# A gather run as one stream, with other transfer shapes, and the product of a quad as one instruction

## The chip, the cores and the metric

The kernel runs on one core of a Trainium2 chip. The metric is the device time of one execution in microseconds (us), lower is better. The engines are TensorE (PE; its weight loads stand as PEld), VectorE (DVE), ScalarE (ACT), GpSimd (POOL) and SyncE (SP), which here only issues transfers to the core's 16 DMA engines.

## What is computed

The reference is a chain of four layers on x of 8 images, 256 channels, 32 x 32 points in float32, each added to x: a selective scan, a mixture of experts, three deformable stages, and a 1x1 convolution. The change is in the deformable stages. Cut to that part:

```python
def _deform(x, ow, ob):
    off = (_conv(x, ow, 1) + ob[None, :, None, None]).reshape(B, C, 2, H, W)
    py = clip(yy + off[:, :, 0], 0, H - 1); px = clip(xx + off[:, :, 1], 0, W - 1)
    y0, x0 = floor(py), floor(px); y1 = minimum(y0 + 1, H - 1); x1 = minimum(x0 + 1, W - 1)
    wy, wx = py - y0, px - x0
    # v00 = x[.., y0, x0] and so on, gathered for each channel and point
    return v00*(1-wy)*(1-wx) + v01*(1-wy)*wx + v10*wy*(1-wx) + v11*wy*wx
h = _bn(_conv(_deform(x, ow1, ob1), w1, 0), ...)     # 256 channels in, 64 out
h = _bn(_conv(_deform(h, ow2, ob2), w2, 1), ...)     # 64 channels
h = _bn(_conv(_deform(h, ow3, ob3), w3, 0), ...)     # 64 channels in, 256 out
```

Every channel has its own sampling positions py and px at each of the 1024 points.

## The kernel before

**No indices are used.** The kernel first takes differences of each image along both axes (`dense`). A sample at (py, px) is then the sum over rows i and columns j of difference(i, j) times clamp(py - i + 1, 0, 1) times clamp(px - j + 1, 0, 1). So a gather is three steps for a channel: row weights, a matmul over i, a product with the column weights, and a sum over j.

**Stages.** `kernel_program` (L1860) runs the scan layer, the experts, `build_offsets_1` (L1149), `load_constants`, and then `build_gather` (g1), `build_middle` (o2), `build_gather` (g2), `build_middle` (o3), `build_gather` (g3) and `build_last`. The offsets stages write four DRAM tensors: `dense` (image differences), `coords` (both coordinates, each split in two parts s whose sum is the float32 value), `whole` (the row coordinate unsplit), and the gather writes `gathered`.

**Quads.** A gather works on sets of 128 channels; g1 has 16 sets, g2 and g3 four each. A set has two halves of 512 points (`NH`), each with 8 quads (`QUADS`), a quad being 16 channels: four units r of 32 partitions times four channels c. So g1 has 256 quads and g2 and g3 64 each, 384 in all. For each quad q:

- Row weights `kw` (128 partitions x 4 x 512: image row on partitions): the coordinate of channel c = 0 of each unit is spread over 32 partitions by a TensorE matmul with `spread` (L1457) and read by ScalarE with a relu (L1401). The coordinates of c = 1 to 3 (`SENT`) come from `whole` by four transfers that each repeat three rows over 32 partitions (`send_rows`, L1346), three buffers deep (`SB`), and VectorE takes the relu of all three (L1423). GpSimd clamps all four at 1 (L1415).
- Row sums: 16 matmuls of 32 x 32 by 512 (L1472; each shows as two records) from `img` and `kw` into four PSUM banks.
- Column weights `vw`: four spread matmuls (L1457) and four relus of ScalarE (L1401), through a ring of three PSUM banks.
- The product (`weigh`, L1434): VectorE multiplies two of the four banks with min(vw, 1), in two instructions per quad. The row matmuls of the next quad wait for both (`weighted`).
- The fold: four matmuls with `fold` (L1482) add over j. After 8 quads ScalarE evacuates the fold bank (L1386) and SyncE stores the half set to `gathered` (L1363).

**Order.** Each engine's order is written out by hand. On VectorE it is product of quad n, then relu of quad n + 2. On TensorE it is row sums of n, three spreads, fold of n - 1, two spreads. The spreads belong to quads n + 1 (`v`) and n + 2 (`k`).

**The loop.** `build_gather` runs a loop over turns of `SETS` = 4 sets; between turns all engines meet at the end of the block. In a turn SyncE issues: rows of quad 0, the loads of set 0, rows of quads 1 and 2, the loads of sets 1, 2 and 3, and then rows of quad 3 and on, each when the relu three quads before is done. The loads of a set (`load_set`) are four transfers of coordinates, 128 partitions x 4 KB each (L1351, 2 MB in all), and after the first of them four of the image, 32 partitions x 32 pieces of 128 bytes each (L1357, 0.5 MB in all).

**The stores** of the stages before: in `build_offsets_1` SyncE stores `dense`, `coords` and `whole`; in `build_middle`, a loop of two turns of four images, per image `dense` (L1638, 64 partitions x 4 KB), two of `coords` (L1642) and `whole` (L1645).

## Time and profile before

| | us |
|---|---|
| median of 3 runs | 5976.52 (5972.13 to 5980.63) |
| the profiled execution | 5969.8, its span 5968.1 |
| TensorE busy | 4860.9 (81% of the span) |
| VectorE busy | 3608.7 (60%) |
| ScalarE busy | 1857.1 (31%) |
| GpSimd busy | 1478.1 (25%) |
| mean granted TensorE clock | 0.887 of full |

The busy shares are means over stages of very different kinds. The sum in the prediction is made against the profiled execution; the median of the runs is 6.7 us above it. A wait is put down by the profile to what ended last before it.

### The profile page before, as it was taken

The numbers are of one execution on the slowest core, as the hardware profiler recorded it, in microseconds if no ns is written. First come the engines' busy times: TensorE is split into PE (matmuls) and PEld (weight loads), VectorE is DVE, ScalarE is ACT, GpSimd is POOL, SyncE is SP. The second block draws the span as 40 slices with busy tenths as digits, with TensorE's granted clock in tenths as the row PEclk, the third lists the DMA queues.
The fourth block names the chain that finished last, engine by engine and source line by source line (L and its number), as shares of the span: only waits on it lengthen the run. The fifth ranks groups of instructions, "written<-read, shape, count | busy, mean of one in ns | idle before, by whom it ended". The sixth has DMA issues, their size and how long they took to land. (4 is left out here: it accounts for less than half of the span.)

```text
span 5968.1 us, 82574 instructions
## 1 busy us (share of the span) xinstructions
PE 4860.9 (81%) x30592; PEld 2689.8 (45%) x30592; DVE 3608.7 (60%) x4317; ACT 1857.1 (31%) x2899; POOL 1478.1 (25%) x1828
## 2 busy tenths in 40 slices
PE   4787887876999799979989994959596983985886
PEld 2333333324777677757767771313131332332222
DVE  6888888875666566652212223848484873863764
ACT  2222222202222122220000003848484751751660
POOL 0222222220000000011101002636363651642540
PEclk7888888867999899989999996979797996997988
DMA  1000000001000000011111119989898968978962
GB/s 30 15 20 17 21 22 21 15 21 65 15 15 8 22 15 15 8 61 74 43 71 74 53 67 193 217 180 218 178 220 181 217 171 183 218 145 143 221 178 91
DMA packets 377577, 558.13 MB, mean 94 GB/s; under 512 B 167464, under 2 KB 169064, under 8 KB 376264
## 3 DMA queue, kind: packets, MB, share of 16 engines
q1 hardware_dynamic: 377160, 552.64, 37.7%
q8 instruction: 253, 4.15, 0.3%
q14 instruction: 164, 1.34, 0.1%
HBM read 439.27 MB, written 113.25 MB: 93 GB/s over the span
## 5 line engine op out<-in xcount | busy, mean ns | idle before, releaser
L1415 POOL TENSOR_SCALAR g_kw<-g_kw 128x512 f32<-128x512 f32 x1536 | 960.8, 650 | 936.7 <-ACT g_kw L1401 637.1
L1401 ACT ACTIVATE g_vw<-ps,l_index 128x512 f32<-128x512 f32 x1536 | 971.0, 686 | 520.4 <-PE ps L1457 520.1
L1434 DVE SCALAR_TENSOR_TENSOR g_prod<-g_vw,ps 128x1024 f32<-128x1024 f32 x768 | 903.3, 1218 | 213.0 <-PE ps L1472 213.0
L1294 PE MATMUL ps<-o_pad,o_ow 128*128 128x512 f32 x3456 | 852.5, 409 | 8.5 <-DVE o_pad L822 7.7
L1457 PE MATMUL ps<-g_coord,l_spread 128*128 128x512 f32 x1920 | 678.5, 452 | 147.6 <-DMA g_coord<-coords 147.4
L1093 PE MATMUL ps<-l_pair,l_w 128*128 128x512 f32 x3072 | 780.3, 403 | 0.0
L1294 PEld LDWEIGHTS ps<-o_pad,o_ow 128*128 128x128 f32 x3456 | 657.3, 191 | 198.0 <-DVE o_pad L822 7.9
L1472 PE MATMUL ps<-g_kw,g_img 32*32 32x512 f32 x12288 | 458.9, 620 | 311.7 <-DVE g_prod L1434 272.5
L1457 PEld LDWEIGHTS ps<-g_coord,l_spread 128*128 128x128 f32 x1920 | 313.1, 194 | 831.1 <-ACT g_vw L1401 615.6
L1093 PEld LDWEIGHTS ps<-l_pair,l_w 128*128 128x128 f32 x3072 | 575.6, 191 | 156.6 <-issue 29.4
L1423 DVE TENSOR_SCALAR g_kw<-g_rows,l_index 128x1536 f32<-128x1536 f32 x384 | 389.8, 1015 | 416.0 <-DMA g_rows<-whole 416.0
L1401 ACT ACTIVATE g_kw<-ps,l_index 128x512 f32<-128x512 f32 x384 | 264.5, 689 | 1098.3 <-PE ps L1457 1081.6
L752 PE MATMUL ps<-l_rows_p,l_sel 72*128 72x512 bf16 x768 | 293.8, 473 | 211.0 <-DVE l_dbx L609 127.2
L1482 PE MATMUL ps<-g_prod,l_fold 128*32 128x512 f32 x3072 | 413.9, 611 | 9.5 <-DVE g_prod L1434 9.5
L1038 DVE TENSOR_TENSOR l_act<-ps,l_act 128x512 f32<-128x512 f32 x256 | 177.0, 691 | 398.0 <-ACT l_act L966 397.5
L428 POOL TENSOR_TENSOR l_acc<-l_acc,l_seen 128x1024 f32<-128x1024 f32 x112 | 283.2, 2528 | 512.9 <-DVE l_seen L619 512.9
L1105 PE MATMUL ps<-l_mixed,l_w 128*128 128x512 f32 x1536 | 401.3, 396 | 3.5 <-DVE l_mixed L822 1.9
L966 ACT ACTIVATE l_act<-ps 128x512 f32<-128x512 f32 x256 | 153.3, 599 | 776.1 <-PE ps L1093 776.1
L130 POOL TENSOR_TENSOR l_moments<-l_moments,l_minus_half 128x2 f32<-128x2 f32 x24 | 16.6, 692 | 1444.2 <-DVE l_moments L99 1444.2
L1105 PEld LDWEIGHTS ps<-l_mixed,l_w 128*128 128x128 f32 x1536 | 287.7, 188 | 79.0 <-issue 7.3
L1472 PEld LDWEIGHTS ps<-g_kw,g_img 32*32 32x32 f32 x12288 | 106.0, 104 | 468.6 <-POOL g_kw L1415 275.6
L1132 DVE SCALAR_TENSOR_TENSOR o_pos<-ps,o_ob,o_grid 128x1024 f32<-128x1024 f32 x32 | 41.1, 1283 | 442.2 <-PE ps L1294 441.9
(247 smaller groups left out, 4911.9 us busy)
## 6 DMA issues: line engine op xcount, KB each, us to landing
g_rows<-whole SPq DMA_DIRECT2D x1536, 192.0 KB, 4.4
g_coord<-coords SPq DMA_DIRECT2D x96, 512.0 KB, 7.2
coords<-o_parts SPq DMA_DIRECT2D x32, 1024.0 KB, 4.0
l_x<-xcur SPq DMA_DIRECT2D x16, 1024.0 KB, 6.5
coords<-o_parts SPq DMA_DIRECT2D x32, 512.0 KB, 5.1
g_img<-dense SPq DMA_DIRECT2D x96, 128.0 KB, 8.6
gathered<-g_res SPq DMA_DIRECT2D x48, 256.0 KB, 4.8
l_xn<-in_x SPq DMA_DIRECT2D x8, 1024.0 KB, 5.0
```

Of the source, the lines that this page charges most:

```text
L428: ins = nc.gpsimd.tensor_tensor(acc[:, h, :], acc[:, h, :], seen[:, i % 2, :], ALU.add)
L752: ins = nc.tensor.matmul(ps[:, lo:lo + HALF], sel[:, q, :], rows_p[:, mine, h, j * HALF:(j + 1) * HALF], start=True, stop=True)
L1093: ins = nc.tensor.matmul(bank(b_ + i % 2), w[:, a, k, e, f * P:(f + 1) * P], pair[:, m % 2, c, k, j * HALF:(j + 1) * HALF], start=(k == 0 ...
L1105: ins = nc.tensor.matmul(bank(5 + c), w2[:, a, f, e, c * P:(c + 1) * P], mixed2[:, i % 3, d, :], start=(e == 0 and f == 0 and r == 0), sto ...
L1294: ins = nc.tensor.matmul(ps[:, lo:lo + HALF], ow[:, a, kk, tap, y, k * P:(k + 1) * P], padded_rows(pad[:, m, c, kk], j, tap), start=(n == ...
L1401: nc.scalar.activation(to, bank(a % RING), ACT.Relu, bias=index[:, 0:1]).then_inc(sem("ring_read"), 1)
L1415: nc.gpsimd.tensor_scalar(part, part, 1.0, 0.0, ALU.min, ALU.max).then_inc(sem("clamped"), 1)
L1423: nc.vector.tensor_scalar(kw[:, q % KB, OWN:4, :].rearrange("p c n -> p (c n)"), rows[:, q % SB].rearrange("p c n -> p (c n)"), index[:, 0 ...
L1434: nc.vector.scalar_tensor_tensor(prod[:, n % PB, 2 * half:2 * half + 2, :].rearrange("p r n -> p (r n)"), vw[:, n % VB, 2 * half:2 * half ...
L1457: nc.tensor.matmul(bank(a % RING), spread[:, int(kind == "v"), h, c, :], coord[:, s, t, j * HALF:(j + 1) * HALF], start=True, stop=True).t ...
L1472: ins = nc.tensor.matmul(ps[c * SIDE:(c + 1) * SIDE, lo:lo + HALF], img[mine, s, g, c, :], kw[mine, n % KB, c, :], start=True, stop=True)
L1482: ins = nc.tensor.matmul(ps[r * SIDE:(r + 1) * SIDE, FOLD_BANK * HALF:(FOLD_BANK + 1) * HALF], fold[:, g, :], prod[:, n % PB, r, :], start ...
```

## The change

`build_gather` loses its loop: all sets of a gather are one block, and 16 sets of g1 are written out. `coord` and `img` hold two sets instead of four and are reused; the loads of set s + 1 are issued while set s runs, after the rows of its quads 7 (image), 8 to 11 (columns) and 12 (row coordinates).

The shapes of transfers change with the layout of the DRAM tensors. The image goes in as four transfers of 32 partitions x 4 KB. The coordinates go in as four transfers of columns, 16 partitions x 4 pieces of 4 KB, and four of rows, 16 partitions x 4 KB, for the two channels of each group of eight whose rows TensorE spreads. Only these row coordinates are loaded. `coord` has 80 partitions, and the spread matmuls contract over 80 rows instead of 128. `whole` holds the three sent channels next to each other, so the rows of a quad are read as one piece of 6 KB (before: three of 2 KB) for each partition, and the four quarters are issued in the order 0, 2, 1, 3. For this the channels of a quad are chosen by `channel_of`, and `spread` and `fold` are built to match.

The product of a quad is one VectorE instruction of 2048 elements over four banks, and waits for all four column weights.

The stages before store `dense` in the new layout, in pieces of 128 bytes, and `build_offsets_1` does so in two transfers per image.

```diff
-SETS = 4
+CROWS = 80
...
                             sp.wait_ge(sem("steps_ready"), KC * (m + 1))
-                            sp.dma_start(dense[bass.ds((b0 + m) * C, C), :].rearrange("(k p) n -> p k n", p=P),
-                                         x[:, m % 2]).then_inc(sem(f"stored{m}"), 16)
+                            for kk in range(KC):
+                                sp.dma_start(dense[bass.ds((b0 + m) * KC + kk, 1)].rearrange("a i p j -> (a p) i j"),
+                                             x[:, m % 2, kk, :].rearrange("p (i j) -> p i j", j=SIDE))\
+                                  .then_inc(sem(f"stored{m}"), 16)
                             if m + 2 < IMGS:
-                                sp.wait_ge(sem(f"stored{m}"), 16)
...
-                        sp.dma_start(coords[bass.ds((b0 + m) * KC + k, 1), y, :, :, :].rearrange("a s p n -> (a p) s n"),
+                        sp.dma_start(coords[bass.ds((b0 + m) * KC + k, 1), y, :, :, :].rearrange("a p s n -> (a p) s n"),
                                      co.stored(slice(0, P), i)).then_inc(sem(f"coords_stored{i}"), 16)
                         if y == 0:
-                            sp.dma_start(whole[bass.ds((b0 + m) * KC + k, 1)].rearrange("a p n -> (a p) n"),
-                                         co.pos[:, i % 2, :]).then_inc(sem(f"coords_stored{i}"), 16)
+                            sp.dma_start(whole[bass.ds((b0 + m) * KC + k, 1)].rearrange("a j p n -> (a p) j n"),
+                                         co.pos[:, i % 2, :].rearrange("p (j n) -> p j n", j=NH)).then_inc(sem(f"coords_stored{i}"), 16)
...
+def channel_of(h, c):
+
+    return h if c == 0 else 2 + 3 * h + c - 1
...
-        coord = st.sb("coord", [P, SETS, 4, N], F32R)
-        img = st.sb("img", [P, SETS, QUADS, 4, SIDE])
+        coord = st.sb("coord", [CROWS, 2, 4, N], F32R)
+        img = st.sb("img", [P, 2, QUADS // 2, 8, SIDE])
-        quads = [(s, j, g) for s in range(SETS) for j in range(NH) for g in range(QUADS)]
-        Q = len(quads)
+        rows = st.sb("rows", [P, SB, 3, HALF])
+        quads = [(s, j, g) for s in range(sets) for j in range(NH) for g in range(QUADS)]
...
-        with nc.Fori(0, blocks // SETS) as turn:
-            n0 = turn * SETS
...
+        with nc.Block() as block:
+
+            @block.sync
+            def _(sp):
+                def send_rows(q):
+                    s, j, g = quads[q]
+                    if q >= SB:
+                        sp.wait_ge(sem("sent_relu"), q - SB + 1)
+                    t, h = divmod(g, 2)
+                    for r in (0, 2, 1, 3):
+                        lo = r * SIDE + 8 * t + channel_of(h, 1)
+                        sp.dma_start(rows[r * SIDE:(r + 1) * SIDE, q % SB].rearrange("p c n -> p (c n)"),
+                                     whole[s, j, lo:lo + 3].rearrange("q n -> (q n)").partition_broadcast(SIDE))\
+                          .then_inc(sem(f"rows_sent{q % SB}"), 16)
+
+                def load_image(s):
+                    if s >= 2:
+                        sp.wait_ge(sem("rows_summed"), PER_SET * (s - 1))
+                    for r in range(4):
+                        mine = slice(r * SIDE, (r + 1) * SIDE)
+                        sp.dma_start(img[mine, s % 2].rearrange("p t q j -> p (t q j)"),
+                                     dense[s, :, mine, :].rearrange("i q j -> i (q j)")).then_inc(sem(f"img_loaded{s % 2}"), 16)
+
+                def load_columns(s, r):
+                    sp.dma_start(coord[16 * r:16 * (r + 1), s % 2].bitcast(F32),
+                                 coords[s, 1, r * SIDE:(r + 1) * SIDE].rearrange("(t q) s n -> (q s) t n", t=4))\
+                      .then_inc(sem(f"coord_loaded{s % 2}"), 16)
+
+                def load_rows(s):
+                    for t in range(4):
+                        sp.dma_start(coord[CM:CROWS, s % 2, t].bitcast(F32),
+                                     coords[s, 0].rearrange("(r t q) s n -> t r q s n", r=4, t=4)[t, :, 0:2]
+                                     .rearrange("r q s n -> r (q s) n")).then_inc(sem(f"coord_loaded{s % 2}"), 16)
+
+                def store(r):
+                    s, j = divmod(r, NH)
+                    sp.wait_ge(sem("res_ready"), r + 1)
+                    sp.dma_start(gathered[s * P:(s + 1) * P, j * HALF:(j + 1) * HALF],
+                                 res[:, r % 2, :]).then_inc(sem(f"stored{r % 2}"), 16)
+
+                send_rows(0)
+                for r in range(4):
+                    load_columns(0, r)
+                load_rows(0)
+                load_image(0)
+                send_rows(1)
+                send_rows(2)
+                for q in range(SB, Q):
+                    send_rows(q)
+                    s, part = divmod(q, PER_SET)
+                    if s + 1 < sets:
+                        if part == 7:
+                            load_image(s + 1)
+                        if 8 <= part < 12:
+                            load_columns(s + 1, part - 8)
+                        if part == 12:
+                            load_rows(s + 1)
+                    if q % QUADS == SB + 2 and q >= QUADS:
+                        store(q // QUADS - 1)
+                store(sets * NH - 1)
+                for r in range(2):
+                    sp.wait_ge(sem(f"stored{r}"), 16 * sets)
...
+                def weigh(n):
+                    dve.wait_ge(sem("rows_summed"), n + 1)
+                    if n >= PB:
+                        dve.wait_ge(sem("folded"), n - PB + 1)
+                    dve.wait_ge(sem("ring_read"), at["v", n, 3] + 1)
+                    nc.vector.scalar_tensor_tensor(prod[:, n % PB].rearrange("p r n -> p (r n)"),
+                                                   vw[:, n % VB].rearrange("p r n -> p (r n)"),
+                                                   1.0, ps[:, ROW_BANK * HALF:(ROW_BANK + 4) * HALF], ALU.min,
+                                                   ALU.mult).then_inc(sem("weighted"), 1)
+
+                for n in range(-2, Q):
+                    if n >= 0:
+                        weigh(n)
+                    if n + 2 < Q:
+                        relu(n + 2)
...
+                    if j == 0 and g == 0:
+                        pe.wait_ge(sem(f"coord_loaded{s % 2}"), 128 * (s // 2 + 1))
+                    nc.tensor.matmul(bank(a % RING), spread[:, h, c if kind == "v" else 4, :],
+                                     coord[:, s % 2, t, j * HALF:(j + 1) * HALF], start=True,
+                                     stop=True).then_inc(sem("ring_filled"), 1)
+
...
+                    if j == 0 and g == 0:
+                        pe.wait_ge(sem(f"img_loaded{s % 2}"), 64 * (s // 2 + 1))
+                    pe.wait_ge(sem("clamped"), 4 * (n + 1))
+                    if n:
+                        pe.wait_ge(sem("weighted"), n)
...
+                            ins = nc.tensor.matmul(ps[c * SIDE:(c + 1) * SIDE, lo:lo + HALF], img[mine, s % 2, g // 2, channel_of(g % 2, c), :],
+                                                   kw[mine, n % KB, c, :], start=True, stop=True)
+                    ins.then_inc(sem("rows_summed"), 1)
...
-                        sp.dma_start(dense[bass.ds(b * CM, CM), :], step[:, m, :]).then_inc(sem("stored"), 16)
+                        part = slice(m % 2 * CM, (m % 2 + 1) * CM)
+                        sp.dma_start(dense[bass.ds(turn * (PASS // 2) + m // 2, 1), :, part, :].rearrange("a i p j -> (a p) i j"),
+                                     step[:, m, :].rearrange("p (i j) -> p i j", j=SIDE)).then_inc(sem("stored"), 16)
                         sp.wait_ge(sem("coords_ready"), m + 1)
                         for y in range(2):
                             half = slice(m % 2 * CM, (m % 2 + 1) * CM)
-                            sp.dma_start(coords[bass.ds(turn * (PASS // 2) + m // 2, 1), y, :, half, :]
-                                         .rearrange("a s p n -> (a p) s n"),
+                            sp.dma_start(coords[bass.ds(turn * (PASS // 2) + m // 2, 1), y, half, :, :]
+                                         .rearrange("a p s n -> (a p) s n"),
                                          co.stored(slice(y * CM, (y + 1) * CM), m)).then_inc(sem(f"coords_stored{m}"), 16)
-                        sp.dma_start(whole[bass.ds(turn * (PASS // 2) + m // 2, 1), half, :].rearrange("a p n -> (a p) n"),
-                                     co.pos[0:CM, m % 2, :]).then_inc(sem(f"coords_stored{m}"), 16)
+                        sp.dma_start(whole[bass.ds(turn * (PASS // 2) + m // 2, 1), :, half, :].rearrange("a j p n -> (a p) j n"),
+                                     co.pos[0:CM, m % 2, :].rearrange("p (j n) -> p j n", j=NH)).then_inc(sem(f"coords_stored{m}"), 16)
...
-        dense = dram("dense", (B * C, N))
+        dense = dram("dense", (B * C // P, SIDE, P, SIDE))
         gathered = dram("gathered", (B * C, N))
-        coords = dram("coords", (B * C // P, 2, 2, P, N))
-        whole = dram("whole", (B * C // P, P, N))
+        coords = dram("coords", (B * C // P, 2, P, 2, N))
+        whole = dram("whole", (B * C // P, NH, P, HALF))
         build_scan_layer(nc, t, ps, xcur)
```

The removed code of the loop body stands in the kernel above. ScalarE's, GpSimd's and TensorE's orders stay, with `weighted` counted once per quad; the constants `spread` and `fold` follow the new channel order.

## Rows read from the trace of the kernel before

**Rows 1.** The page: span, and DMA share of each of 40 slices
```profile
span 5968.1 us, 82574 instructions
DMA  1000000001000000011111119989898968978962
```

**Rows 2.** Timeline of SyncE's queue (start us, us, engine, line, operation): stage bounds
```profile
3610.10 1.88 SPq L1346 DMA_DIRECT2D g_rows<-whole  x4
...
4875.49 2.16 SPq L1628 DMA_DIRECT2D o_x<-gathered  x4
...
5004.64 1.77 SPq L1346 DMA_DIRECT2D g_rows<-whole  x4
...
5319.34 16.09 SPq L1633 DMA_DIRECT2D o_x<-gathered  x8
...
5473.62 1.75 SPq L1346 DMA_DIRECT2D g_rows<-whole  x4
...
5787.81 0.55 SPq L1759 DMA_DIRECT2D l_h<-gathered  x1
```

**Rows 3.** Timeline of all engines, one steady quad of the first gather
```profile
3703.21 2.35 DVE L1434 SCALAR_TENSOR_TENSOR g_prod<-g_vw,ps 128x1024 f32<-128x1024 f32 x2 [0.53 <-PE ps L1472]
...
3704.87 0.74 PE L1457 MATMUL ps<-g_coord,l_spread 128*128 128x512 f32 x2
...
3705.48 1.01 DVE L1423 TENSOR_SCALAR g_kw<-g_rows,l_index 128x1536 f32<-128x1536 f32 x1
...
3705.71 1.15 PE L1472 MATMUL ps<-g_kw,g_img 32*32 32x512 f32 x32
3705.99 0.68 ACT L1401 ACTIVATE g_vw<-ps,l_index 128x512 f32<-128x512 f32 x1
...
3707.03 2.35 DVE L1434 SCALAR_TENSOR_TENSOR g_prod<-g_vw,ps 128x1024 f32<-128x1024 f32 x2 [0.53 <-PE ps L1472]
```

**Rows 4.** Timelines of VectorE and SyncE's queue, first turn's end, second turn's head
```profile
3913.29 2.35 DVE L1434 SCALAR_TENSOR_TENSOR g_prod<-g_vw,ps 128x1024 f32<-128x1024 f32 x2 [1.47 <-PE ps L1472]
...
3926.95 3.03 SPq L1346 DMA_DIRECT2D g_rows<-whole  x4
...
3933.72 1.02 DVE L1423 TENSOR_SCALAR g_kw<-g_rows,l_index 128x1536 f32<-128x1536 f32 x1 [18.09 <-DMA g_rows<-whole]
...
3949.99 1.02 DVE L1423 TENSOR_SCALAR g_kw<-g_rows,l_index 128x1536 f32<-128x1536 f32 x1 [15.25 <-DMA g_rows<-whole]
3950.92 2.35 DVE L1434 SCALAR_TENSOR_TENSOR g_prod<-g_vw,ps 128x1024 f32<-128x1024 f32 x2
...
3995.56 1.02 DVE L1423 TENSOR_SCALAR g_kw<-g_rows,l_index 128x1536 f32<-128x1536 f32 x1 [37.60 <-DMA g_rows<-whole]
```

**Rows 5.** Windows: stretch, us, busy us of engines, granted clock, DMA share, GB/s
```profile
3956.00:3995.00 39.00, 7.00 (x58) 1.96 (x56) 1.96 (x2) 6.22 (x10) 1.41 (x3) 0.59 1.10 211
...
4004.00:4060.00 56.00, 54.53 (x671) 17.87 (x673) 47.38 (x44) 46.50 (x76) 36.92 (x59) 1.00 0.97 221
4060.00:4120.00 60.00, 58.36 (x718) 18.91 (x711) 51.58 (x48) 50.15 (x82) 39.23 (x63) 1.00 0.91 215
```

**Rows 6.** The page's groups of instructions: shape, count, busy us, mean ns
```profile
L1434 DVE SCALAR_TENSOR_TENSOR g_prod<-g_vw,ps 128x1024 f32<-128x1024 f32 x768 | 903.3, 1218 | 213.0 <-PE ps L1472 213.0
...
L1038 DVE TENSOR_TENSOR l_act<-ps,l_act 128x512 f32<-128x512 f32 x256 | 177.0, 691 | 398.0 <-ACT l_act L966 397.5
```

**Rows 7.** The page: instruction queues (packets, MB), and rows issues (KB each, us to landing)
```profile
q8 instruction: 253, 4.15, 0.3%
q14 instruction: 164, 1.34, 0.1%
...
g_rows<-whole SPq DMA_DIRECT2D x1536, 192.0 KB, 4.4
```

**Rows 8.** Timeline of SyncE's queue: an image load, and stores of a middle stage
```profile
3930.98 4.93 SPq L1357 DMA_DIRECT2D g_img<-dense  x4
...
4926.56 2.03 SPq L1638 DMA_DIRECT2D dense<-o_step  x1
4929.99 1.45 SPq L1642 DMA_DIRECT2D coords<-o_parts  x2
```

259 lines of the change are left out of this document (95 added, 164 removed).

## The prediction

> **What bounds the kernel now.** I read the slices of the span first. From about 60% on, where the three gathers lie, the DMA share is 8 or 9 tenths, and under 2 tenths in most slices before them [rows 1]. So the changed part is a stretch in which 16 DMA engines are nearly full, and a gain in VectorE alone can be lost there.
>
> Next, SyncE's queue gives the stages their bounds [rows 2]. The first gather runs from 3610.10 to 4875.49 us, 1265.4 us for four turns of the loop; the second from 5004.64 to 5319.34, 314.7; the third from 5473.62 to 5787.81, 314.2. Together 1894.3 us for 384 quads (24 blocks of 128 channels, 16 quads each).
>
> Inside a turn there are two regimes. The steady one repeats every 3.82 us: product starts at 3703.21 and 3707.03 [rows 3]. Its loop is: two products on VectorE (2.35 us), 0.15 us later the row matmuls into the four banks that the products had been reading (first start 3705.71), then the next product. The relu of the sent rows (1.01 us) lies in the shadow of those matmuls. 64 quads at 3.82 us are 244.5 us, but a turn takes 316.3. The rest stands in front of three relus: 18.09, 15.25 and 37.60 us, all waiting for transferred rows [rows 4], 70.9 us in sum. They are at the head of the turn: SyncE issues the loads of four sets before the rows of quad 3, and those rows queue behind all the bytes. In this stall the DMA share is 1.10 at 211 GB/s, so it is a full queue and no latency; a few microseconds later, with the same queue full of rows, it is 0.97 at 221 GB/s, and in calm running 0.91 at 215 [rows 5]. I take 221 GB/s and 215 / 0.91 = 236 GB/s as the two bounds of what these engines can carry. The share can exceed 1, so it is a rough scale.
>
> **The change, part by part.** *One stream.* The first gather loses three of four stage heads, and sets 1 to 3 of every turn are no longer loaded ahead of quad 3. What one stream still pays: the head, 24.0 us from first issue (3926.95) to first product (3950.92), and the tail, 11.3 us from the last product's end (3913.29 + 2.35) to the next turn's first issue [rows 4]. In front of the first product the queue now has rows 0.79 MB, coordinates 1.31, image 0.52 and rows 0.79, 3.4 MB where it had 4.2 (all four coordinate pieces were 2.1 MB), so I take 20 us for the head. With an allowance of 3 us for the first quads, which run at a lower granted clock (0.59 in the stall, 1.00 in calm running [rows 5]), a stream costs 34 us beside its quads, three streams 102 us.
>
> *The product.* A product of 1024 elements takes 1218 ns, an elementwise operation of 512 from the same kind of memory 691 [rows 6], so 1.03 ns an element and about 2272 ns for 2048, against 2350 for the pair: 0.08 us less per quad, 31 us over 384, if VectorE stays the bound. It may now start only when all four weight tiles are in; the last one ends at 3706.67 and the product starts at 3707.03 [rows 3], so 0.36 us cover that, and if the cover went, ScalarE would be late next. TensorE's last two spread matmuls end by their rows at 3705.61, 0.10 us ahead of the row matmuls, so about 0.1 us is all that a shorter product can bring. Period with VectorE as the bound: 3.74 us.
>
> *Bytes.* Here is the step that decides. Per quad the stream moves 4 x 196,608 = 786,432 bytes of rows and, over eight quads, a store of 262,144: 819,200 bytes, or 215 GB/s at 3.82 us, which is the rate of the calm window. Until now the loads of the sets were outside the steady part. They now run inside it: columns 1,048,576, row coordinates 262,144, image 524,288 bytes per set of 16 quads, 114,688 per quad. The coordinates were 2,097,152 per set and shrink. Sum 933,888 bytes per quad. At 3.74 us this would need 250 GB/s; the engines carry 221 to 236. So the period becomes 933,888 / 221 = 4.23 us or 933,888 / 236 = 3.96 us. I take **4.05 us**: pieces of 6 KB instead of 2 KB, 4 KB instead of 128 bytes in the image, and the quarters in the order 0, 2, 1, 3 should bring a little and not nothing. The lower bound of these unknown effects is the VectorE period of 3.74.
>
> By the Trainium skill, SBUF — State Buffer, section Door 1: The DMA port swizzle, 32 partitions reach 8 of 16 ports (asymptote about 218 GB/s), and partitions 64 and up are on the other 8. The trace agrees for the rows: 221 GB/s with the queue full. The same page says under "Can I just issue two DMAs to hit both halves?" that two transfers to different halves gained 6% over one. By that the new order would give 221 x 1.06 = 234 GB/s and 3.99 us, inside my bounds.
>
> *Waits that are added.* The image load of set s+1 waits for the end of set s-1's last row sum; SyncE reaches it after the rows of that set's seventh quad, whose own wait is later, so it is free. The row coordinates of a set are issued some seven quads ahead of their first matmul, 28 us; a landing of rows takes 4.4 us [rows 7] and up to three quads are queued, so it holds. A late one would stop TensorE, then everything. The unrolled first gather fetches no more code: the two instruction queues carried 4.15 + 1.34 MB for 82,574 instructions, 66 bytes for each one executed, so a loop saved none [rows 1, 7].
>
> *The stores of the image.* `dense` is now written in pieces of 128 bytes, 2048 per image in the middle stages and 4096 per half image in the first offsets stage. In the latter TensorE's matmuls cover them. In the former the last one is issued at 4926.56, takes 2.03 us, and the next store of coordinates goes out at 4929.99 [rows 8], 1.4 us of slack. Loading an image in 128-byte pieces took SyncE 1.2 us per 1024 pieces at the head of a turn (4.93 us for four) [rows 8], so 2048 take about 2.5 us and the landing a few more: 0 to 4 us in each of four turns, I take 1.5, 6 us. Nothing is gained there.
>
> **Sum.** 384 x 4.05 = 1555, with 102 for heads and tails 1657, against 1894: -237. With +6 the profiled execution of 5969.8 us becomes 5739. The median of the runs is 6.7 us above that execution, so I say **5745 us**. The likeliest case alone runs from 3.96 us (5710) to 4.23 (5814).
>
> **Rivals.** *VectorE stays the bound (chance 0.22).* Larger pieces and the alternating quarters lift the transfers over 250 GB/s. For it: in calm running the share is 0.91, so the engines finish early. Against: with a full queue of rows they carried 221 GB/s [rows 5]. Period 3.74 to 3.85: 5626 to 5668 us. The columns' pieces may then collide for a few quads only.
>
> *The narrow column loads (chance 0.15, and slower 0.05).* A columns transfer fills 16 partitions, a rows transfer 32, the old coordinates all 128. If the rate falls with the partitions, 1.05 MB per set at half of 221 GB/s costs 4.7 us more per set, 0.30 us a quad: 4.53 us from the poor bound, 4.35 from mine, 5860 us. The point of no gain is (1894 - 102 - 6) / 384 = 4.65 us, 0.60 us a quad over my value or 9.6 us per set. At a third of the rate the columns cost 9.5 us more, at a quarter 14.2: period 4.94, 6087 us, **slower than before**, with the place at quads 8 to 12 of each set and VectorE's relu waiting there. Against it: three quads of rows are queued ahead and soak up part of it.
>
> By the same section of that page 16 partitions reach 4 ports and 104 GB/s at 1 MiB; that gives 10.1 us per set for the columns, 5.4 more than at 221, and 4.39 us from my value, 5875 us. No row here shows a 16-partition transfer.
>
> *The part "over all DMA engines" changes nothing (inside the likeliest).* The old coordinate loads already had the share at 1.10, so they used all engines; then fewer bytes are the only gain there, as the sum assumes.
>
> **How the numbers follow.** DMA-bound near 4.05: 0.55; VectorE-bound: 0.22; narrow loads but still a gain: 0.15; slower by them: 0.05; between, within 0.2% of before: 0.03. The measurement of this kernel tells about 0.2% from no change. Range: from the VectorE case at 3.75 to the narrow case at 4.35, 5630 to 5860, which leaves out about 2 in 10.
>
> **What would show it.** Right: period of the products near 4.0 us on average, 3.74 when rows are there, relus waiting for rows in the second half of each set; DMA share near 1 at 225 to 235 GB/s over the whole gather; one product of about 2.27 us; no stall of 15 or 37 us after the first quads. Wrong: a calm period of 3.74 without waits (the transfers were faster than I think), or waits of more than 10 us at every quad 8 to 12 (narrow loads), or stages 2 and 3 longer than 315 us.

## The result, and the profile after

The changed kernel takes 5919.0 us (median of 4 runs, 5896.16 to 5933.34), the kernel before 5978.1 beside it: a ratio of 0.990, 95% interval 0.986 to 0.993. It is faster by 1%, 59 us where the prediction said 231, and above the top of the range (5860). The profiled execution is one of 5933.34 us, span 5931.7. Page of the changed kernel, to be read against [rows 1, 6, 7]:

```profile
span 5931.7 us, 79284 instructions
PEclk7888888867999899998999997987887887787887
DMA  1000000001000000002211216998887967877872
...
L1453 DVE SCALAR_TENSOR_TENSOR g_prod<-g_vw,ps 128x2048 f32<-128x2048 f32 x384 | 877.9, 2286 | 295.1 <-PE ps L1490 294.9
...
L1444 DVE TENSOR_SCALAR g_kw<-g_rows,l_index 128x1536 f32<-128x1536 f32 x384 | 392.5, 1022 | 320.6 <-DMA g_rows<-whole 318.7
...
g_rows<-whole SPq DMA_DIRECT2D x1536, 192.0 KB, 4.9
```

The product is one instruction of 2286 ns. The DMA share in the gathers has not risen to full, it is 8 to 9 tenths and then 7 and 8; and the granted clock in those slices is 7 and 8 tenths but for one slice with 9. VectorE still waits 318.7 us for rows. The bounds of the three gathers, in SyncE's queue of the changed kernel, answer to [rows 2]:

```profile
3616.64 1.72 SPq L1349 DMA_DIRECT2D g_rows<-whole  x4
...
4832.99 2.17 SPq L1646 DMA_DIRECT2D o_x<-gathered  x4
...
4963.13 1.75 SPq L1349 DMA_DIRECT2D g_rows<-whole  x4
...
5292.24 15.60 SPq L1651 DMA_DIRECT2D o_x<-gathered  x8
...
5447.76 1.73 SPq L1349 DMA_DIRECT2D g_rows<-whole  x4
...
5755.25 0.57 SPq L1779 DMA_DIRECT2D l_h<-gathered  x1
```

The first gather takes 1216.4 us (49 less than before), the second 329.1 (14 more), the third 307.5 (7 less): 1853.0 us in all, 41 less, where the prediction had 237 less. In the first, 24.6 us pass from the first issue to a first product at 3641.25, and 8.4 from the start of the last product (4824.62) to the next stage. Without three times these 33 us, 1754 us are left for 381 intervals between products, 4.60 us each. The prediction had 4.05, and its point of no gain at 4.65.

Where an interval of 3.75 becomes one of 4.60 is seen in VectorE's timeline of the changed kernel, here in the third set, whose last product starts at 3852.71, and the start of the fourth (in brackets the idle time before an instruction, and what ended it):

```profile
3804.39 2.29 DVE L1453 SCALAR_TENSOR_TENSOR g_prod<-g_vw,ps 128x2048 f32<-128x2048 f32 x1 [0.54 <-PE ps L1490]
...
3808.14 2.29 DVE L1453 SCALAR_TENSOR_TENSOR g_prod<-g_vw,ps 128x2048 f32<-128x2048 f32 x1 [0.40 <-PE ps L1490]
3812.54 1.02 DVE L1444 TENSOR_SCALAR g_kw<-g_rows,l_index 128x1536 f32<-128x1536 f32 x1 [2.12 <-DMA g_rows<-whole]
...
3818.28 1.02 DVE L1444 TENSOR_SCALAR g_kw<-g_rows,l_index 128x1536 f32<-128x1536 f32 x1 [2.52 <-DMA g_rows<-whole]
...
3823.77 1.02 DVE L1444 TENSOR_SCALAR g_kw<-g_rows,l_index 128x1536 f32<-128x1536 f32 x1 [2.27 <-DMA g_rows<-whole]
...
3828.36 1.02 DVE L1444 TENSOR_SCALAR g_kw<-g_rows,l_index 128x1536 f32<-128x1536 f32 x1 [1.38 <-DMA g_rows<-whole]
...
3835.20 1.02 DVE L1444 TENSOR_SCALAR g_kw<-g_rows,l_index 128x1536 f32<-128x1536 f32 x1 [3.62 <-DMA g_rows<-whole]
...
3846.18 2.29 DVE L1453 SCALAR_TENSOR_TENSOR g_prod<-g_vw,ps 128x2048 f32<-128x2048 f32 x1 [3.07 <-PE ps L1490]
...
3852.71 2.29 DVE L1453 SCALAR_TENSOR_TENSOR g_prod<-g_vw,ps 128x2048 f32<-128x2048 f32 x1 [3.31 <-PE ps L1490]
...
3859.25 2.29 DVE L1453 SCALAR_TENSOR_TENSOR g_prod<-g_vw,ps 128x2048 f32<-128x2048 f32 x1 [3.32 <-PE ps L1490]
3861.45 1.01 DVE L1444 TENSOR_SCALAR g_kw<-g_rows,l_index 128x1536 f32<-128x1536 f32 x1
3863.54 2.29 DVE L1453 SCALAR_TENSOR_TENSOR g_prod<-g_vw,ps 128x2048 f32<-128x2048 f32 x1 [1.07 <-PE ps L1490]
```

Three regimes stand here. First the calm one, 3804.39 to 3808.14, 3.75 us. Then five relus in a row wait 1.4 to 3.6 us for rows: they hold back the products of quads 8 to 12, counted from 0, just after the columns of the next set were issued (3798.12 to 3809.51 in SyncE's queue). And then, with the rows there, three products wait 3.1 to 3.3 us for TensorE and start about 6.5 us apart. Windows of the changed kernel over the same stretch say why (columns: stretch, us, busy PE, PEld, DVE, ACT, POOL, granted clock, DMA share, GB/s):

```profile
3800.00:3808.00 8.00, 7.91 (x113) 2.54 (x91) 6.62 (x5) 6.56 (x11) 5.41 (x9) 1.00 1.03 193
3816.00:3824.00 8.00, 8.00 (x78) 2.28 (x78) 3.45 (x3) 3.10 (x5) 2.38 (x4) 0.57 0.99 181
3840.00:3848.00 8.00, 8.00 (x52) 2.33 (x54) 4.93 (x3) 4.36 (x8) 3.65 (x7) 0.50 0.87 218
3848.00:3856.00 8.00, 8.00 (x54) 1.92 (x46) 4.61 (x4) 3.70 (x7) 2.34 (x4) 0.50 0.35 104
3864.00:3872.00 8.00, 7.89 (x96) 2.59 (x98) 6.93 (x5) 6.69 (x12) 5.43 (x10) 1.00 0.88 230
```

Finer windows of the same stretch show when the clock falls:

```profile
3812.00:3816.00 4.00, 2.37 (x26) 0.76 (x33) 3.22 (x2) 3.59 (x6) 2.34 (x4) 1.00 1.13 213
3816.00:3820.00 4.00, 4.00 (x39) 1.20 (x42) 1.72 (x2) 1.34 (x3) 0.62 (x2) 0.51 0.91 182
3824.00:3828.00 4.00, 3.17 (x45) 0.92 (x43) 2.99 (x2) 3.11 (x5) 2.38 (x4) 1.00 1.01 223
3836.00:3840.00 4.00, 1.43 (x34) 0.58 (x35) 3.57 (x4) 0.50 (x1) 2.80 (x5) 1.00 0.78 227
3840.00:3844.00 4.00, 4.00 (x17) 1.04 (x15) 3.10 (x2) 2.19 (x4) 1.31 (x3) 0.50 0.92 224
```

It does not take five waits. After the first of them, in which TensorE is busy for 2.37 of 4 us, the granted clock stands at 0.51 (3816 to 3820), next to 0.50, the lower of its two levels, 1.2 GHz. From 3824 on it is at 1.00 again, although relus still wait. After the longest wait, with TensorE busy for 1.43 of 4 us, it is at 0.50 once more (3840). There TensorE is busy without a break and passes one quad in 6.5 us; the DMA engines, with all three row buffers full, drop to a share of 0.35. At 3864 the clock is back at 1.00 and the calm regime with it.

I sorted all intervals between products by their length, as the timeline gives them. Of 381, 221 are calm (3.75 us). 48 are of the kind of 6.5 us and cost 133.5 us over 3.752 each. The other 112 are mostly waits for rows, some of them already at a falling clock, and cost 188.8 us. So per quad about 0.5 us of waits and 0.35 us of low clock: 3.75 + 0.85 = 4.60.

The length alone does not separate the two causes cleanly. Of the 48 intervals, 11 also hold a relu that waits over 1 us for rows, and 7 lie among the first eight intervals of a gather, where the clock is low before any load of a next set is issued. Sorted by what is waited for instead, 93 intervals with such a relu wait cost 181 us, and 67 without one cost 141 us, of which 25 us lie at the heads of the three gathers.

### The profile page after: what moved, and what is told of

Read it like the earlier page. It is cut to its first block and busy times, and to the rows that moved or that the text cites. A ratio compares the mean times of both kernels' runs of the same rounds, so it can differ in the third digit from the quotient of the medians.

```text
span 5931.7 us, 79284 instructions
## 1 busy us (share of the span) xinstructions
PE 5069.3 (85%) x30592; PEld 2742.2 (46%) x30592; DVE 3585.2 (60%) x3933; ACT 1854.0 (31%) x2899; POOL 1449.0 (24%) x1828
## 5 line engine op out<-in xcount | busy, mean ns | idle before, releaser
L1436 POOL TENSOR_SCALAR g_kw<-g_kw 128x512 f32<-128x512 f32 x1536 | 931.6, 630 | 931.6 <-ACT g_kw L1422 690.8
L1453 DVE SCALAR_TENSOR_TENSOR g_prod<-g_vw,ps 128x2048 f32<-128x2048 f32 x384 | 877.9, 2286 | 295.1 <-PE ps L1490 294.9
L1475 PE MATMUL ps<-g_coord,l_spread 80*128 80x512 f32 x1920 | 758.3, 498 | 123.4 <-DMA g_coord<-coords 123.4
L1475 PEld LDWEIGHTS ps<-g_coord,l_spread 80*128 80x128 f32 x1920 | 351.2, 218 | 924.9 <-ACT g_vw L1422 702.7
L1490 PE MATMUL ps<-g_kw,g_img 32*32 32x512 f32 x12288 | 520.6, 704 | 106.6 <-DVE g_prod L1453 93.6
L1444 DVE TENSOR_SCALAR g_kw<-g_rows,l_index 128x1536 f32<-128x1536 f32 x384 | 392.5, 1022 | 320.6 <-DMA g_rows<-whole 318.7
L1500 PE MATMUL ps<-g_prod,l_fold 128*32 128x512 f32 x3072 | 477.4, 696 | 4.6 <-DVE g_prod L1453 4.5
L613 DVE TENSOR_TENSOR_SCAN l_states<-ps,l_dbx 128x1024 f32<-128x1024 f32 x128 | 293.2, 2290 | 23.3 <-PE ps L752 19.5
```

The source lines that it names most:

```text
L613: nc.vector.tensor_tensor_scan(states[:, i % 2, :], ps[:, 0:2 * HALF], dbx[:, i % 2, :], 0.0, ALU.mult, ALU.add).then_inc(sem("da_used"), 1)
L1436: nc.gpsimd.tensor_scalar(part, part, 1.0, 0.0, ALU.min, ALU.max).then_inc(sem("clamped"), 1)
L1444: nc.vector.tensor_scalar(kw[:, q % KB, 1:4, :].rearrange("p c n -> p (c n)"), rows[:, q % SB].rearrange("p c n -> p (c n)"), index[:, 0:1 ...
L1453: nc.vector.scalar_tensor_tensor(prod[:, n % PB].rearrange("p r n -> p (r n)"), vw[:, n % VB].rearrange("p r n -> p (r n)"), 1.0, ps[:, RO ...
L1475: nc.tensor.matmul(bank(a % RING), spread[:, h, c if kind == "v" else 4, :], coord[:, s % 2, t, j * HALF:(j + 1) * HALF], start=True, stop ...
L1490: ins = nc.tensor.matmul(ps[c * SIDE:(c + 1) * SIDE, lo:lo + HALF], img[mine, s % 2, g // 2, channel_of(g % 2, c), :], kw[mine, n % KB, c, ...
```

## The experiments

All times are medians beside runs of the kernel before on the same chip (5972.7 to 5978.6 us), with the ratio to it. "Low quads" are the intervals of 6.4 to 6.7 us, counted from each run's timeline.

### Where the loss sits

**Without the loads.** Only the first two sets of a gather load their image, columns and the row coordinates that TensorE spreads, and all later sets use these; the rows of every quad are still sent. So this kernel leaves out the loads of the later sets and gathers from the wrong images.

```diff
-                    if s + 1 < sets:
+                    if s == 0:
                         if part == 7:
                             load_image(s + 1)
```

> The changed kernel without the loads of image and coordinates for the sets from the third on; these sets compute with the first two sets' data, rows are still sent. Theory L (the loads inside the stream cause the waits and, behind them, the low TensorE clock): nearly all quads at 3.75 us, 1440 + 100 us for the three gathers, some 310 us less than the changed kernel: about 5600 to 5640 us (g2 and g3 keep the load of their second set: 10 to 20 us above). Theory R (rows alone fill the engines and the waits come from them): over 5750 us. Theory C (the clock falls for another reason): quads of 6.5 us remain without a wait before them.

Measured: 5676.8 us, ratio 0.950 (0.947 to 0.952), 242 us below the changed kernel. The first gather takes 1008.3 us. Of the waits for rows 113.5 us are left, 92 of them ahead of the first products of the three gathers; between products they are 21 us, where the changed kernel has 227. There are 14 low quads. The window 3700 to 4600 us of this kernel:

```profile
3700.00:4600.00 900.00, 887.88 (x10723) 290.60 (x10722) 768.93 (x478) 755.55 (x1223) 586.00 (x955) 1.00 0.83 220
```

The rows alone flow at VectorE's period with a DMA share of 0.83, at the granted clock 1.00. The whole shortfall against the prediction lies in what the loads inside the stream do. This run doesn't tell whether it is their bytes or their form, since it takes away both; and at 5676.8 us it is slower than the 5600 to 5640 us that I expected.

**The quarters in the order 0, 1, 2, 3.**

```diff
-                    for r in (0, 2, 1, 3):
+                    for r in range(4):
```

> The changed kernel with the four quarters of a quad's rows issued in the order 0, 1, 2, 3 again. Theory P (two halves of the partitions have write paths of their own, and alternating between them lets transfers overlap): the rows fall back from 240-250 GB/s in a full queue to about 221, each set of 16 quads takes 4 to 6 us more, 24 sets make 100 to 150 us: 6020 to 6070 us, and relus wait for rows in the calm half of a set too. Theory D (the order does nothing, the larger pieces made the rows faster): 5900 to 5935 us, as the changed kernel.

Measured: 6010.0 us, 1.004 (1.002 to 1.007): 91 us above the changed kernel and slower than before. VectorE waits 410.2 us for rows instead of 318.7, and the window 3700 to 4600 us carries 194 GB/s instead of 199. I had given the order "a little and not nothing"; without it there is no gain at all. The time lies just under the 6020 to 6070 us expected if the order counts, and far from the 5900 to 5935 us expected if it doesn't.

**The columns over a wider span.** Each columns transfer goes to every fourth of 64 partitions instead of 16 neighbouring ones; `spread` follows.

```diff
-                    sp.dma_start(coord[16 * r:16 * (r + 1), s % 2].bitcast(F32),
+                    sp.dma_start(coord[r:CM:4, s % 2].bitcast(F32),
```

> The changed kernel with each columns transfer into every fourth of 64 partitions instead of 16 neighbours, weights permuted to match; bytes, pieces and times of issue stay. Theory N (a transfer into 16 neighbouring partitions has few write paths and runs at 110 to 150 GB/s, which holds up the rows behind it): the waits at quads 8 to 12 shrink by over a third, some 1 us per columns transfer, 4 us a set, 96 us, and part of the clock loss behind them: 5780 to 5850 us. Theory M (the mean rate of all engines is the bound): no change, 5900 to 5935.

Measured: 5847.9 us, 0.978 (0.975 to 0.981), 71 us below the changed kernel. The waits for rows fall from 318.7 to 199.3 us with the same bytes in the same number of pieces, at the same place. Only the partitions that they reach are others.

**Two products per quad** in the changed kernel, each waiting for its own two weight tiles as before.

> The changed kernel with the product of a quad as two instructions of two banks again. If VectorE's loop sets the period only where rows are there (221 of 384 intervals were at 3.75 us), the period there returns to 3.82, 0.065 us x 221 = 14 us slower: 5925 to 5940 us. If the transfers were the bound everywhere, no difference. If the single instruction cost cover elsewhere (ScalarE's last weights come late), this is faster than 5910.

Measured: 5934.2 us, 0.993 (0.991 to 0.996). The intervals of the two ratios overlap, and ten runs of this kernel spread over 90 us (5882 to 5972), so of the one product's worth in total nothing can be told here. Its calm intervals are back at 3.82 us, 247 of them.

**The kernel before with the one product** alone.

> The kernel before with the one instruction over four banks alone. My sum: period 3.75 instead of 3.82 us in the steady part, 353 of 384 intervals, 22 us less: 5950 to 5960 us. If the transfers (share 0.91 to 0.97) take over as the bound there, no change: 5970 to 5980.

Measured: 5957.4 us, 0.997 (0.996 to 0.998), some 20 us less. The page of this kernel shows the product at 2288 ns, and 352 intervals stand at 3.75 us instead of 3.82.

### Bunching, depth and width

**The pieces spread out.** Columns, row coordinates and image go one piece at a time after the rows of quads 5 to 12 of each set.

```diff
-                    if s + 1 < sets:
-                        if part == 7:
...
+                    if s + 1 < sets and 5 <= part < 13:
+                        k = part - 5
+                        if k % 2 == 0:
+                            load_columns(s + 1, k // 2)
+                        else:
+                            load_rows(s + 1, k // 2)
+                            load_image(s + 1, k // 2)
```

> The changed kernel with the same loads of the next set in another order of issue: one columns transfer after the rows of quads 5, 7, 9, 11 each, one row-coordinate and one image transfer after those of quads 6, 8, 10, 12 (before: image after 7, columns after 8 to 11, all four row-coordinate transfers after 12). Theory B (bursts: the mean load fits, the bunching does not, since only three quads of rows are queued ahead): the waits shrink by half and the low-clock quads with them: 5760 to 5830 us. Theory S (a stall of 2.5 us per columns transfer is there whatever its place): within 20 us of the changed kernel, 5890 to 5935.

Measured: 5933.2 us, 0.991 (0.987 to 0.995): no change against the changed kernel. So with narrow pieces and three buffers it isn't the bunching; each piece costs about the same wherever it is put.

**Four row buffers** (`SB` = 4) in the changed kernel.

> The changed kernel with four buffers for the sent rows instead of three, nothing else. Theory B (bursts): one more quad of rows ahead hides 3.75 us of each set's 8 to 10 us of waits, and the clock falls less often: 5780 to 5860 us. Theory M (mean rate): the queue is only longer, 5890 to 5935.

Measured: 5869.3 us, 0.981 (0.977 to 0.985), 50 us less, between the two expected ranges; waits for rows 227.5 us. With the pieces spread as well:

> The changed kernel with four buffers of rows and the pieces of a set's load issued after quads 5 to 12, the narrow transfers kept. Theory W (width): about as with four buffers alone, 5850 to 5890 us. Theory B (bursts): with one more quad ahead the spread pieces hide, 5700 to 5780.

Measured: 5864.7 us, 0.981 (0.977 to 0.985), the same. Depth soaks up part of each disturbance, spreading adds nothing to it.

**Row coordinates over a wider span.** They come in one transfer of 64 partitions, with matrices of their own to spread them (`spread_k`), instead of four of 16 partitions; the columns stay narrow.

```diff
-                    for t in range(4):
-                        sp.dma_start(coord[CM:CROWS, s % 2, t].bitcast(F32),
...
+                    sp.dma_start(rowco[:, s % 2].bitcast(F32),
```

> The changed kernel with the row coordinates of a set in one transfer of 64 partitions from a source of outer size 16, instead of four of 16 partitions from a source of outer size 4, which show as 4 KB packets on a few engines only; the spread matmul of a row coordinate has weights of its own for it. If these four transfers hold up a share of the engines for 4 to 5 us a set (the longest relu wait of a set, 3.1 to 3.7 us, stands behind them), 24 x 3 us plus a part of the clock loss are won: 5800 to 5860 us. If a few engines being late costs nothing, 5890 to 5935.

Measured: 6015.9 us, 1.007 (1.004 to 1.009), a clear miss. The groups of waits of this kernel, and under them those of the changed kernel:

```profile
DVE g_prod L1454 <- PE ps L1492: 443.0, 313, 3.3
DVE g_kw L1445 <- DMA g_rows<-whole: 245.4, 90, 17.7
```

```profile
DVE g_kw L1444 <- DMA g_rows<-whole: 318.7, 111, 17.4
DVE g_prod L1453 <- PE ps L1490: 294.9, 291, 3.3
```

The waits for rows did fall, by 73 us. But the waits for TensorE rose by 148: 84 low quads instead of 48, 233 us instead of 134, and a granted clock of 0.79 from 3700 to 4600 us where it was 0.83. Fewer waits, and a longer time. In windows of 1 us from 3650 to 4625 us (low is a granted clock under 0.75) the clock doesn't fall more often here, it stays low longer: 10 stretches with 433 us in all, where the changed kernel has 17 with 319. Why it stays down longer I can't say.

**Both spans wide**, three buffers, pieces not spread.

> The changed kernel with both widenings (columns into every fourth of 64 partitions, row coordinates in one transfer of 64 partitions), three buffers of rows and the bunched order of issue kept. Theory W (the width of the transfers is nearly the whole loss): 5670 to 5730 us. Theory B (depth and order count as much): 5760 to 5810.

Measured: 5709.8 us, 0.956 (0.955 to 0.957), 209 us less than the changed kernel, where the columns alone brought 71. The worths don't add up from the single changes, since the row coordinates alone cost 97. And the row coordinates' change is more than a wider span: they also come in one transfer instead of four. Only the columns' run changes nothing but the partitions reached.

**All of it**: four buffers, columns and row coordinates wide, pieces spread.

> The changed kernel with four buffers of sent rows, columns into every fourth of 64 partitions, the loads of a set in pieces after quads 5 to 12, and the row coordinates of a set in one transfer of 64 partitions (before: four of 16 partitions whose source has an outer size of 4), spread by a matmul with weights of their own. If bursts and narrow transfers are the whole loss against the kernel without loads (5677 us), this comes within 30 us of it: 5680 to 5710 us. If the mean rate binds beside them, 5740 or more: 24 sets x 16 quads at 4.0 us.

Measured: 5659.0 us, 0.947 (0.945 to 0.948). This is the fastest kernel of the study, 319 us below the kernel before and 260 below the changed one, and 21 us under the range that I expected. Its window 3700 to 4600 us:

```profile
3700.00:4600.00 900.00, 885.78 (x10707) 288.06 (x10707) 764.80 (x476) 754.22 (x1219) 584.27 (x949) 1.00 1.00 246
```

VectorE's busy 764.80 us is what it was without the loads (768.93): the stream runs at VectorE's period with all its bytes, and the engines carry 246 GB/s over 900 us. All of its 17 low quads lie among the first eight intervals of the three gathers, 47 us with no wait for rows behind them.

### What the clock costs by itself

**Pauses.** In the combined kernel VectorE writes an unused tile once in each of quads 8 to 12 of a set, 120 times in all. Rows are not late: between products relus wait 0.5 us for them in all.

```diff
+                    if n >= 0 and 8 <= n % PER_SET < 13:
...
+                        nc.vector.memset(pause[:, :], 0.0).then_inc(sem("paused"), 1)
```

> The best kernel so far (5659 us: four buffers, wide transfers, spread pieces; its quads run at 3.75 us with the TensorE clock at 1.00) with a pause of VectorE, a fill of 2400 elements of a buffer of its own, about 2.55 us, between product and relu of five neighbouring quads of each set, 120 in all; no transfer is changed. It puts waits like those of the changed kernel there without their cause. The pauses alone stretch an interval from 3.75 to some 5.7 us: 120 x 1.95 = 235 us, 5890 to 5900 us. Theory K (such waits make the granted clock of TensorE fall, and the next three or four quads take 6.5 us): quads of 6.5 us appear after them and it takes 5980 to 6060 us. If the clock needs another cause (a load of the memory, the matmuls themselves), 5880 to 5910 us and all quads at 3.75 outside the pauses.

Measured: 6121.6 us, 1.025 (1.021 to 1.028), 463 us more than without the pauses, and above the 5980 to 6060 us that I expected even if such pauses bring the clock down. Its timeline of VectorE shows what one pause costs by itself:

```profile
3781.24 2.27 DVE L1459 SCALAR_TENSOR_TENSOR g_prod<-g_vw,ps 128x2048 f32<-128x2048 f32 x1
3783.97 2.06 DVE L1471 MEMSET g_pause<- 128x2400 f32 x1 [0.45 <-issue]
3785.94 0.90 DVE L1450 TENSOR_SCALAR g_kw<-g_rows,l_index 128x1536 f32<-128x1536 f32 x1
3786.75 2.27 DVE L1459 SCALAR_TENSOR_TENSOR g_prod<-g_vw,ps 128x2048 f32<-128x2048 f32 x1
```

An interval of 5.51 us instead of 3.75, so 120 x 1.76 = 211 us. The other 250 us are low quads: 109 with 302 us, where the combined kernel has 17 with 47. Waits for rows are no part of it (72.6 us, as without the pauses, and nearly all in the heads). The clock falls with the first pause, which starts at 3778.45:

```profile
3776.00:3780.00 4.00, 3.95 (x47) 1.21 (x46) 3.55 (x2) 3.83 (x7) 2.72 (x4) 1.00 1.04 228
3780.00:3784.00 4.00, 2.19 (x27) 0.73 (x42) 3.55 (x4) 2.88 (x5) 4.00 (x5) 0.99 0.92 224
3784.00:3788.00 4.00, 4.00 (x43) 1.03 (x11) 4.00 (x3) 1.64 (x3) 1.17 (x3) 0.50 0.56 157
```

TensorE is busy for 2.19 of the 4 us from 3780 on, and at 3784 the clock is at 0.50. In the second to fifteenth set of the first gather it falls 5 to 8 us after the start of the first pause in eleven cases, and 10 to 12 us after it, behind the second pause, in three. So a short idle time of TensorE is followed by the low clock without any late transfer, and the low clock costs more than the idle time.

### Which part lifted the rate

The prediction held that the engines carry 221 to 236 GB/s. They carried 246. Two parts of the change could have done it.

**The combined kernel with the order 0, 1, 2, 3.**

> The combined kernel (four row buffers, wide columns, wide row coordinates, pieces spread) with the quarters of each quad's rows issued 0, 1, 2, 3. Its stream needs 249 GB/s at VectorE's period of 3.75 us. Theory O (the alternating order is what lets the engines carry more than my bound of 236 GB/s): the window 3700 to 4600 us shows 221 to 236 GB/s and the period is 3.96 to 4.23 us; 384 quads by 0.2 to 0.5 us more, and the clock falls in some of the waits: 5750 to 5900 us. Theory P (the 6-KB pieces do it, the order matters only where narrow transfers disturb the queue): 5660 to 5700 us, the window at 240 GB/s or more.

Measured: 5734.1 us, 0.960 (0.958 to 0.962), 75 us more, just under the 5750 to 5900 us expected if the order counts. Relus wait for rows 26 times (89.4 us) instead of 9 times (73.1), and there are 27 low quads instead of 17, 28 us of the 75.

**The combined kernel with padded row buffers**, so that the rows land in pieces of 2 KB:

> The combined kernel with the row buffers padded by 8 elements per channel, so that a quad's rows go in pieces of 2 KB instead of 6 KB as before the change; bytes and order stay. Theory O: no change beyond 20 us, 5650 to 5680 us. Theory P: the rate falls to the old 221 to 236 GB/s, 5750 to 5900 us. If both count, both this run and the one with the plain order lose part of it.

Measured: 5723.0 us, 0.957 (0.955 to 0.958), 64 us more, but not by the transfers. The groups by line show the relu at 1807 ns instead of 1014:

```profile
L1449 DVE TENSOR_SCALAR g_kw<-g_rows,l_index 128x1536 f32<-128x1536 f32 x383 | 692.1, 1807 | 69.6 <-DMA g_rows<-whole 69.6
```

With it a period of 3.92 us, 0.17 above 3.75, 384 x 0.17 = 65 us. This run tells nothing of the pieces, so another pads the DRAM tensor instead: **2-KB pieces, the relu as it was.**

```diff
-        whole = dram("whole", (B * C // P, NH, P, HALF))
+        whole = dram("whole", (B * C // P, NH, P, HALF + 8))
```

> The padded row buffers of the run before made VectorE's relu slower (1807 ns instead of 1022), which by itself set a period of 3.92 us and explains its 64 us, so the size of the pieces was not tested. Here the DRAM tensor with the row coordinates is padded instead: the rows of the combined kernel are read in pieces of 2 KB into the same buffers, and the relu stays as it was. If the pieces count (theory P), the rate falls below the 249 GB/s that the period of 3.75 us needs: the window 3700 to 4600 us at 236 to 243 GB/s, 5690 to 5760 us. If they don't, 5650 to 5675 us with the window at 245 GB/s or more, and the order of the quarters is what lifted the rate.

Measured: 5662.3 us, 0.947 (0.945 to 0.949), no change against the combined kernel, though the queue carried 370,008 packets instead of 271,704. Windows 3700 to 4600 us, first of the kernel with the plain order, then of the one with 2-KB pieces:

```profile
3700.00:4600.00 900.00, 874.36 (x10231) 280.61 (x10216) 731.14 (x454) 719.86 (x1165) 559.67 (x909) 0.97 0.99 236
```

```profile
3700.00:4600.00 900.00, 884.63 (x10706) 287.85 (x10676) 764.56 (x476) 752.81 (x1219) 584.53 (x952) 1.00 1.04 247
```

In the plain order the engines carry 236 GB/s at a share of 0.99, the stream needs 933,888 bytes in 3.75 us, 249 GB/s, and runs short of rows. In the order 0, 2, 1, 3 they carry 246 to 247 in either size of piece. So the order does it, 28 of the 75 us by way of the low clock (0.97 in that window). The size makes no difference to the time here, but 246 and 247 GB/s are again what VectorE asked for: the share is 1.04 with the small pieces and 1.00 with the large, and no run shows what either could carry beyond that.

**The kernel before with the order 0, 2, 1, 3.**

> The kernel before with the quarters of the rows issued 0, 2, 1, 3 and nothing else. Its steady part is bound by VectorE, so theory O gives only the heads of the turns back in part: the three waits of 70.9 us in sum, at a full queue, shrink by the ratio 221 to 246, some 7 us in each of 6 turns, 5930 to 5950 us. Theory P gives 5965 to 5985 us, no change.

Measured: 5974.8 us, 0.999 (0.998 to 1.000). No gain, and not the 30 to 50 us that I expected of the order at the heads of the turns. There the queue holds the old coordinate and image loads: in this kernel 3956 to 3995 us still shows 212 GB/s, before 211 [rows 5]. The waits for rows fall by 12 us only, from 416.0 to 403.7. I read this as an order that pays where rows fill the queue and VectorE wants more of them than the plain order gives; no run tests it further.

## Why the prediction was wrong

**The step that failed** is "So the period becomes 933,888 / 221 = 4.23 us or 933,888 / 236 = 3.96 us. I take 4.05 us". The period was 4.60, and the gathers took 1853 us where the sum has 1657. Two things were wrong in it, on opposite sides.

*The cap was no cap.* 221 and 215 / 0.91 = 236 GB/s were read from a stream bound by VectorE, so they say what it asked for, not what the engines could give; and the 211 GB/s at a share of 1.10 belonged to another mix of transfers. With the narrow transfers out of the way the rate was 246 and the stream VectorE's. So even at its best the step would have named the wrong bound, and the rival in which VectorE stays the bound had the right rate.

*The mean hid the loss.* I divided all bytes by one rate. In the run the columns and row coordinates of a set go to 16 partitions each and hold up rows that are only three quads deep. A mean over 16 quads leaves no such wait. That the time is in these loads is shown by taking them away (242 us less); that it isn't in their bytes, by the combined kernel, which moves them all and takes 260 us less. That width is part of it is shown by the columns over a wider span (71 us less). With the row coordinates in one wide transfer as well it is 209, in which width and the number of transfers are not separated.

**A term was missing**: the granted clock. The prediction gave it 3 us per stream, at the head. In the changed kernel intervals without a late row cost 141 us, 25 of them at the heads and about 116 behind the waits, where the waits themselves cost 181. The pauses show it with no late transfer in play. It is also why even the narrow rival, with its 4.35 to 4.53 us, was too low: calm period and waits make 3.75 + 0.5 = 4.25 us, and the clock makes it 4.60.

**Point by point.** *Head and tail:* in the first gather 24.6 us and, from the last product's end, 6.1 us, for 20 and 11.3; its first quads cost 3.9 us for the 3 allowed. 34.6 for 34, right in sum, with the head too small and the tail too large. In the other two gathers the first quads cost 8.8 and 12.6 us, so the three streams take 119 us beside their quads, not 102. *The product:* 2286 ns for 2272; calm period 3.75 for 3.74; alone on the kernel before some 20 us less, for 31 promised: about 0.06 us went from each of 352 calm intervals, nothing from the others. *Stores of the image:* predicted 6 us; the two middle stages between the gathers take 130.1 and 155.5 us where they took 129.2 and 154.3, 2 us in all. The first gather begins 6.5 us later than before, which nothing in the sum had: the prediction put the stores of the first offsets stage at nothing ("TensorE's matmuls cover them"), and no run here separates what the 6.5 us are. *Waits added:* none was late, as said: TensorE waits for coordinates three times, once at the head of each gather, and never inside a stream. *The narrow column loads:* the place was right to the quad ("quads 8 to 12 of each set", with "VectorE's relu waiting there"), and I gave it 0.20 in all and put the likeliest case elsewhere. "Three quads of rows are queued ahead and soak up part of it" was true but weak; a fourth is worth 50 us. Its sign of being wrong, waits of more than 10 us at these quads, was met only by their sum: in the set shown five waits of 1.4 to 3.6 us, 11.9 in all. *The rule on ports:* the Trainium skill, SBUF — State Buffer, Door 1: The DMA port swizzle, says that a transfer's partitions set how many ports it reaches, and that 16 neighbours reach four. The runs agree in direction, since the columns' span alone brought 71 us. Where the prediction says that the trace agrees with that page's 218 GB/s for 32 partitions, it rests on the 221, a demand; with rows in transfers of 32 partitions the combined kernel carried 246. The same page's 6% for two transfers to different halves (section "Can I just issue two DMAs to hit both halves?") I put on 221 GB/s. The order moved 236 to 246, 4% or more, since 246 is where VectorE takes over; put on 236 the rule would have given 250 and thus the VectorE period. No run here shows the ports themselves.

**What stays open.** Why the clock stays low so much longer with the wide row coordinates alone (84 low quads for 48), while both spans together bring fewer (29); how much of their gain is width and how much the single transfer; what the spread pieces and the fourth buffer are worth each once both are wide; and why the second gather lost 14 us where the third won 7.

## What to carry to other kernels

A rate read in a stretch that another engine bounds is a demand; the capacity is known only where the consumer waits. When transfers of another shape are moved into a stream, cost each by how long it holds up what is queued behind it, against the depth of the buffers, and not as bytes in a mean. Try them over more partitions, and the stream's own transfers in another order of partitions; spreading the narrow ones in time brought nothing here. And count a short recurring wait in front of TensorE twice, once for itself and once for the quads at the low clock that follow.

## What the hardware showed that I had not expected

- One short wait can bring the granted clock from 1.00 to 0.50: behind the first late relu (TensorE busy 2.37 of 4 us) and behind the first pause (2.19 of 4 us). While it is down a quad takes 6.5 us instead of 3.75, though every input is there. In the first gather of the changed kernel it comes back after 3 to 45 us, and can do so while relus still wait (3824 to 3840). In the pauses' run 120 pauses worth 211 us cost 463.
- The order in which four quarters of one tile are issued, with the same bytes and pieces, is 236 against 246 GB/s or more, 75 us of this kernel, 91 us of the changed one.
- A VectorE relu of 128 x 1536 elements takes 1014 ns from one run of memory and 1807 ns when its source has a gap of 8 elements after every 512 (source and target are then written as three rows of 512).
- 98,304 more packets in the queue, rows of 2 KB for 6 KB, cost nothing that can be measured at 246 to 247 GB/s.
